# The gated experts' down products: from one f32 product to a sum of three f16 products

## What is computed

```python
# layer 1, "attention": a recurrence, one step for each token
h[t] = tanh(Wi @ ln(x[t]) + bi + Wh @ h[t-1] + bh);   x = x + h
# layer 1, ffn: one shared expert of 512 hidden columns and 16 routed ones of 64, 4 of them for a token
hidden = silu(xn @ gate) * (xn @ up)          # 1536 hidden columns in all
hidden[:, 512:] *= weight_of_the_token_for_the_expert   # 0 where it isn't chosen
x = x + hidden @ down                         # down: 1536 x 256
```

## Time and profile before

| what | us |
|---|---|
| median of three runs | 1479.22 (1477.72 to 1484.81) |
| the profiled execution | 1469.44 |
| its span, first to last instruction | 1467.7 |
| mean granted clock of PE | 0.987 |
| PE busy | 1420.8 (97%) |
| DVE busy | 806.5 (55%) |
| ACT busy | 594.2 (40%) |
| L1648, the down products, busy on PE | 113.4 |
| L535, fillers, busy on PE | 149.8 |

### The profile page before, as it was taken

How to read it: one execution, slowest core, us unless ns; L and a number is a source line. 1 busy time by engine, 2 the same in 40 slices (tenths; PEclk the granted TensorE clock), 3 DMA queues, 4 the chain that set the end, 5 groups by cost and what they waited for, 6 DMA issues and landing times.

```text
span 1467.7 us, 48130 instructions
## 1 busy us (share of the span) xinstructions
PE 1420.8 (97%) x19734; PEld 1006.2 (69%) x19734; DVE 806.5 (55%) x2574; ACT 594.2 (40%) x2778; POOL 38.0 (3%) x60
## 2 busy tenths in 40 slices
PE   5699899999999999999999999999999999999998
PEld 4466367777777777776776777777767677766555
DVE  6636864287854126967572225766444653455473
ACT  2052223734314784342248874551342334332310
POOL 1000000000000000000000000000000000000000
PEclk9799999999999999999999999999999999999999
DMA  5734100110000002110000002310000100002000
GB/s 160 143 79 107 38 2 2 23 41 3 2 2 3 2 4 43 35 25 3 2 3 3 3 3 90 94 25 1 2 2 15 39 3 2 16 2 38 16 1 15
DMA packets 45468, 40.17 MB, mean 27 GB/s; under 512 B 9723, under 2 KB 44486, under 8 KB 45254
## 3 DMA queue, kind: packets, MB, share of 16 engines
q1 hardware_dynamic: 43526, 36.32, 10.5%
q10 hardware_dynamic: 1728, 0.79, 0.5%
HBM read 25.81 MB, written 10.80 MB: 25 GB/s over the span
## 4 chain that ended last, share of the span: by engine, by line
PE 92%; DVE 4%; DMA 2%; SPq 1%; issue 0%; ACT 0%; DVEq 0%; ACTq 0%
PE b L516 22%; PE b L1596 9%; PE b L1376 9%; PE b L535 7%; PE b L1648 7%; PE b L1004 6%; PE b L975 5%; PE b L741 4%; PE b L920 4%; PE b L697 3%; DVE mx L929 3%; PE b L1257 2%; PE b L1232 2%; PE b L652 2%; PE b L1193 1%; PE b L459 1%
## 5 line engine op out<-in xcount | busy, mean ns | idle before, releaser
L516 PEld LDWEIGHTS b<-hp,whp 128*128 128x128 f16 x12276 | 482.2, 96 | 255.9 <-ACT hp L561 147.7
L516 PE MATMUL b<-hp,whp 128*128 128x2 f16 x12276 | 538.3, 165 | 1.8 <-ACT hp L561 0.5
L567 DVE TENSOR_TENSOR hp<-hist,hp 128x4 f16<-128x4 f32 x1023 | 165.5, 162 | 449.4 <-ACT hist L562 439.6
L561 ACT ACTIVATE hp<-b 128x4 f16<-128x4 f32 x1024 | 177.9, 174 | 511.5 <-PE b L516 499.2
L929 DVE TENSOR_REDUCE mx<-b 128x1 f32<-128x512 f32 (+3 forms) x304 | 188.3, 653 | 2.5 <-PE b L923 1.5
L989 ACT ACTIVATE vp<-b 128x512 f32<-128x512 f32 x288 | 170.8, 601 | 21.3 <-PE b L978 13.2
L562 ACT ACTIVATE hist<-b 128x4 f32<-128x4 f32 x1024 | 177.2, 173 | 0.0
L1596 PE MATMUL b<-vp,heads 128*128 128x512 f16 x576 | 159.9, 378 | 0.0
L535 PE MATMUL b<-whp 128*128 128x512 f16 (+7 forms) x562 | 149.8, 339 | 0.0
L1376 PE MATMUL b<-we,xT 128*128 128x256 f32 x512 | 147.7, 405 | 0.0
L920 PE MATMUL b<-heads 128*128 128x512 f16 (+3 forms) x384 | 112.6, 331 | 5.9 <-DVE mx L929 2.4
(11 more groups left out here) (203 smaller groups left out, 1573.4 us busy)
## 6 DMA issues: line engine op xcount, KB each, us to landing
x_qs<-qx_scr SPq DMA_DIRECT2D x48, 128.0 KB
qx_scr<-xq_pair SPq DMA_DIRECT2D x16, 256.0 KB, 2.1
heads<-q_scr SPq DMA_DIRECT2D x24, 128.0 KB, 4.4
heads<-k_scr SPq DMA_DIRECT2D x36, 64.0 KB, 2.6
x<-in_x SPq DMA_DIRECT2D x8, 256.0 KB, 6.4
q_scr<-tail SPq DMA_DIRECT2D x8, 256.0 KB, 2.3
k_scr<-tail SPq DMA_DIRECT2D x8, 256.0 KB, 2.3
we<-in_L_ffn_We SPq DMA_DIRECT2D x2, 1024.0 KB
```

Of the source, the lines that this page charges most:

```text
L516: return pe.matmul(self.z(t)[:, m], self.w.whp[:, a, k, m * P:(m + 1) * P], self.g.hp16[:, (t - 1) % 2, part, k, :], start=False, stop=Tru ...
L561: act.activation(self.g.hp16[:, t % 2, 0], self.z(t), ACT.Tanh, scale=1 / LIFT).then_inc(self.s["hi_ready"], 1)
```

## The change

A down product becomes three f16 products of 256 columns: high part of the hidden block with high part of `wd`, high with low, and low with high. `update` multiplies the sum by 1/64 while it adds. For each of the 48 blocks there are two new instructions: `keep_hidden` on ACT copies hT into its f16 high part, and `hidden_low` on DVE makes the f16 rest. The new pairs have three buffers `hp` in `heads`. `product` now waits for the block's `hidden_low` of three blocks before, and the new copy for its down products. The planner's cost for a down product goes from 0.43 to 0.33, with 0.52 and 0.6 for the new kinds.

The down matrix is loaded into another part of `heads` and split like the gate and up weights: four more `split_high` and four more `split_low`, 128x768 each.

Many semaphores that count one thing each are merged into a few (`filled`, `filled_v`, `prepared`, `ctx_in`), with the counts in the waits changed to match. Two waits change in what they wait for: the cast of the mask waits for all four loads of its group and not for the mask alone, and so does all that waited for three of them.

```diff
-        st.add("pe", "gat_down", self.down, n * MH * TC, 0.43, lambda i: rank(i // (MH * TC)) + 0.25,
+        st.add("act", "gat_hh", self.keep_hidden, n * MH, 0.52, of_block(0.245))
+        st.add("v", "gat_hl", self.hidden_low, n * MH, 0.6, of_block(0.246))
+        st.add("pe", "gat_down", self.down, n * MH * TC, 0.33, lambda i: rank(i // (MH * TC)) + 0.25,
...
     def product(self, v, i):
         if i >= 3:
-            v.wait_ge(self.s["down"], i - 2)
+            v.wait_ge(self.s["hl"], i - 2)
...
+    def keep_hidden(self, act, n):
+        c, m = self.blocks[n]
+        if m < MS:
+            act.wait_ge(self.s["hm"], n + 1)
+        else:
+            act.wait_ge(self.s["hc"], NR * c + m - MS + 1)
+        if n >= 3:
+            act.wait_ge(self.s["down"], n - 2)
+        act.activation(self.hp[:, n % 3, 0, :], self.hT[:, n % 3, :], ACT.Copy).then_inc(self.s["hh"], 1)
+
+    def hidden_low(self, v, n):
+        v.wait_ge(self.s["hh"], n + 1)
+        v.tensor_tensor(self.hp[:, n % 3, 1, :], self.hT[:, n % 3, :], self.hp[:, n % 3, 0, :], ALU.subtract
+                        ).then_inc(self.s["hl"], 1)
...
     def down(self, pe, i):
-        if p == 0 and m < MS:
-            pe.wait_ge(self.s["hm"], n + 1)
-        if p == 0 and m >= MS:
-            pe.wait_ge(self.s["hc"], NR * c + m - MS + 1)
-        last = pe.matmul(o[:, D * (p % 2):D * (p % 2) + D], self.hT[:, n % 3, P * p:P * p + P], self.w.wd[:, m, :],
-                         start=m == 0 and p % 2 == 0, stop=m == MH - 1, skip_group_check=True)
+        if i == 0:
+            pe.wait_ge(self.w.s["whole_split"], 12)
+        if p == 0:
+            pe.wait_ge(self.s["hl"], n + 1)
+        for at, (h, wd) in enumerate(((0, self.w.wd_hi), (0, self.w.wd_lo), (1, self.w.wd_hi))):
+            last = pe.matmul(o[:, D * (p % 2):D * (p % 2) + D], self.hp[:, n % 3, h, P * p:P * p + P], wd[:, m, :],
+                             start=m == 0 and p % 2 == 0 and at == 0, stop=m == MH - 1 and at == 2, skip_group_check=True)
...
     def update(self, v, j):
-        v.tensor_tensor(x, self.st.bank("gat_d", j // TC, p // 2)[:, D * (p % 2):D * (p % 2) + D], x, ALU.add
-                        ).then_inc(self.s["fx"], 1)
+        v.scalar_tensor_tensor(out=x, in0=self.st.bank("gat_d", j // TC, p // 2)[:, D * (p % 2):D * (p % 2) + D],
+                               scalar=1 / LIFT, in1=x, op0=ALU.mult, op1=ALU.add).then_inc(self.s["fx"], 1)
...
         def split_high(act, i):
+            if j == 2:
+                act.wait_ge(*w.gated_in)
+                act.activation(w.wd_hi[:, wd_part(i)], wd_whole[:, wd_part(i)], ACT.Copy, scale=LIFT
+                               ).then_inc(s["whole_high"], 1)
+                return
...
         def split_low(v, i):
+            if j == 2:
+                v.scalar_tensor_tensor(out=w.wd_lo[:, wd_part(i)], in0=wd_whole[:, wd_part(i)], scalar=LIFT,
+                                       in1=w.wd_hi[:, wd_part(i)], op0=ALU.mult, op1=ALU.subtract
+                                       ).then_inc(s["whole_split"], 1)
+                return
...
             if i == 2:
-                v.wait_ge(s["mask8_in"], 16)
-                v.tensor_copy(wx0.mask_row[:], mask8[:]).then_inc(s["mask_in"], 1)
+                v.wait_ge(s["ctx_in"], 64)
+                v.tensor_copy(wx0.mask_row[:], mask8[:]).then_inc(s["filled_v"], 1)
...
-        st.add("act", "split_high", split_high, 8, 0.8, lambda i: 1000)
-        st.add("v", "split_low", split_low, 8, 0.85, lambda i: 1000)
+        st.add("act", "split_high", split_high, 12, 0.8, lambda i: 1000)
+        st.add("v", "split_low", split_low, 12, 0.85, lambda i: 1000)
```

More of the change, by code:

```diff
@@ L1121, in rows_k @@
         sp.wait_ge(self.s["zeroed"], layer + 1)
-        sp.wait_ge(*w.rows_in)
+        for sem, count in w.rows_in:
+            sp.wait_ge(sem, count)
         rows = self.s[f"k_rows{layer}"]
@@ L1420, in __init__ @@
         self.ov = out.rearrange("(t p) d -> p t d", p=P)
-        self.s = st.sems("gat", "xh xl logits ex chain cT cph cpl cleared made th sv hm spread hc down fx stored")
+        self.s = st.sems("gat", "xh xl logits ex chain cT cph cpl cleared made th sv hm spread hc hh hl down fx stored")
         n = NK
@@ L1746, in all_layers @@
         wx1.bo, wx1.one_row, wx1.ones16 = sb("bo", [1, D]), sb("one_row", [1, P]), wx0.ones16
-        wx1.mask_in, wx1.rows_in, wx1.early = None, (s["rows"], 2), 200
+        wx1.mask_in, wx1.rows_in, wx1.early = None, wx0.rows_in, 200
         wx1.ctx_in, wx1.q_in, wx1.w_in = (s["ctx1_in"], 80), (s["q1_in"], 64), (s["q1_in"], 64)
-        w.wd, w.w_hi, w.w_lo = vp[:, 0:3072].rearrange("p (m n) -> p m n", m=MH), w_parts[0:2], w_parts[2:4]
+        w.wd_hi, w.wd_lo = (vp[:, 1536 * k:1536 * k + 1536].bitcast(F16).rearrange("p (m n) -> p m n", m=MH) for k in range(2))
+        w.w_hi, w.w_lo = w_parts[0:2], w_parts[2:4]
         w.gated_in = (s["w_in"], 48)
@@ L1962, in guard_cross @@
         def guard_cross(act):
-            act.wait_ge(s["lifted"], 1)
-            act.wait_ge(s["b_in"], 1)
-            act.wait_ge(s["w_lo"], 1)
+            act.wait_ge(s["prepared"], 3)
         def guard_rnn(act):
```

57 lines of the change are left out of this document (30 added, 27 removed).

## The result

The changed kernel takes 1461.32 us (median of six runs, 1454.39 to 1468.54) against 1478.84 us for the kernel before in the same comparison: a ratio of 0.9875, 95% interval 0.9833 to 0.9917. The profiled execution took 1454.39 us with a span of 1451.4. It is the fastest of the six, as the one before (1469.44) was faster than its median.

The account below looks back on a forecast made before the run. PE's queue, with down products on the recurrence's path, was taken as the bound after the standstill. Terms +5.5 - 15.7 + 1 - 3.2 = -12.4 us from the 1479.22 us median gave 1466.8 us, range 1456 to 1480.

Parts of the forecast that it names:

- Part 1: Start of the kernel, merged semaphores: the later cast of the mask is absorbed, 0 us, at most 1 us.
- Part 2: Standstill of the recurrence, waiting for layer 0's last chunk: added splits, copies and subtractions lengthen it 5.5 us (3.8 to 7.5).
- Part 3: 281 steps after the standstill: shorter down products on PE's queue, 293.1 to 277.4 us, -15.7 (-8 to -22).
- The low end of my range: 281 steps: only raw PE time goes and a third lands in gaps free anyway, -8 us.
- The new instructions: 23 ScalarE copies and 22 VectorE subtractions in the 281 steps: taken as 0, 7 us if the cover is gone.
- Part 4: Last step to last chunk's experts: five shorter blocks give -3.2 us, late work costs up to 4.1, sum +1.
- Part 5: Last chunk's experts: routing ends later but blocks are shorter, 56.5 to 53.3 us, -3.2 (-6 to -1).
- (b): Rival, no gain: the recurrence refills PE's gaps with fillers, -1.5 us in sum, 1478 us; chance 0.19.
- (a): Rival, bigger saving: all 281 steps reach their kind's shortest length, -22 us in sum, 1457 us; chance 0.15.
- (c): Rival, slower: new copies and subtractions delay the recurrence's tanh or subtraction, 1489 us at 0.5 us each; chance 0.07.
- (d): Rival, slower: weight loads can't overlap products, so a down product takes 0.61 us, 1504 us; chance 0.02.
- The median: Whole kernel: the change was put on the shown runs' median of 1479.22 us, giving 1466.8 us.

Follow-up runs that it names:

- sems_only: The kernel before with only the merged semaphores and their wait counts, down products still f32: 1482.4 us, ratio 1.0026.
- late_split: The changed kernel with the four down-matrix splits on ScalarE and VectorE ordered behind the last layer-0 chunk's highest-score reductions: 1457.01 us, ratio 0.9817.
- double_copies: The changed kernel, same order, with each keep_hidden copy and hidden_low subtraction issued twice, the extra into a spare buffer: 1487.71 us, ratio 1.0018.

## Why the prediction held, step by step

- **Part 1**, 0: right, shown by sems_only at full clock. The start's -4.1 us against the profile before is scatter: the profiles run here have their first step between 224.7 and 230.9 us.
- **Part 2**, +5.5: +4.7. The place was right, and of the 4.7 us that I gave the splits late_split shows 4.2. What I laid on top for the gated blocks' copies and subtractions was too much; between the splits and the standstill DVE sits idle 0.6 to 0.9 us in many of the steps, which is room for them.
- **Part 3**, -15.7: -17.0, and -18.3 at full clock. By classes: two f16 products in the long gap 27 x 0.955 (priced 0.98), the other 33 steps with down products 33.5 us (34), makes 93.2 (94.9), of which 1.4 is half clock, the rest 123.7 (122.1). The reason was right and is shown from both sides: the products alone in the old order give -12.6 us over 60 of 63 steps, and f32 products in the new order take 12.3 of the 17.0 back. The other 4.7 us are the order's, which the forecast held in its kinds of steps without naming it: there are fewer down products (88 for 94), and two together in the long gap cost 0.09 us less than one in each gap, 2.5 us over 27 steps. How the rest splits isn't measured. The low end of my range, raw time only, was no real bound: beside the recurrence an f32 product costs 0.148 us more, not 0.105.
- **The new instructions**, 0: right. 23 steps with the copy grew by 0.24 us in sum, 22 or 23 with the subtraction by 0.4 to 0.8, by how finely the kinds are cut, against the shortest step of their kind. The 0.16 us a copy was to cost in a step of 0.785 us did not come: three of the 23 copies stand in such steps, the others in steps of 0.84 us and more.
- **Part 4**, +1: +0.6, from two larger terms of opposite sign, as priced: the product alone gives -3.8 (priced -3.2), the copies, subtractions and the new order take 4.4 (4.1). How that splits between the three isn't measured.
- **Part 5**, -3.2: -2.7. The turn came at +22.5 us and the next down product at +28.0 (priced 22.5 and 28.3). The block was mis-sized: 4.32 us, not 4.20. The 1.84 us from L1648's start to the next makes already held the f32 weight load that I took off once more: the first of the eight f32 records starts 0.32 us ahead of the second, the others 0.216 from each other.
- **Rivals.** (b) would have needed the fillers to eat the gain: they did grow by 18.7 us, and the 281 steps became shorter all the same. (a) wanted 22 us in the 281 steps, where 17.0 came, 18.3 at full clock. The measured median lies about midway between the forecast and (a), but the forecast's terms each hold within 1.3 us. (c) and (d) fell in the runs above.
- **The median.** The time came out 5.5 us under the forecast, more than any part's error. The terms of the sum measured -14.4 in place of -12.4. Two stages that I had at 0 add -1.8: the start's scatter (-4.1) and the clock in the steps up to 740 (+2.3). Moving the difference of two profiles to the medians of a few runs adds the last 1.6: the spans differ by 16.3 and the medians by 17.5, and the kernel before was 1478.84 here and not 1479.22. That these went the same way is chance. That there was nothing to be had from the clock was read rightly off the stages of one profile, but half clock moves other runs of these kernels by more than any one of Parts 2, 4 and 5.

## What to carry to other kernels

Busy time of a product says little where another loop shares the engine: look for rows in which that loop holds exactly one, two or none of them, and price the change by the distance between the loop's rows. Don't take it that three products cost more than one: here an f16 product of 256 columns takes 0.109 us from start to start and an f32 one 0.43, and beside a run of tiny products the three were cheaper by 0.148 us, not by 0.105. When work is added for a conversion, ask first what stands behind it in each queue at the one place where everything waits: the four weight splits cost 4.2 us in front of the reductions and at most 0.5 behind them.

## What the hardware showed that I had not expected

**The scatter between runs goes with TensorE's clock.** In every profile the granted clock is 1.00 nearly everywhere, and 0.50 (1.2 in place of 2.4 GHz) in stretches of 3 to 21 us: in sum some 8 us behind 220 us in the kernel before, 22 in the changed one, 47 in sems_only, 69 in double_copies. Of the ten runs of the changed kernel those with mean clocks of 0.989 and 0.987 took 1453.5 and 1454.4 us, those with 0.973 and 0.974 took 1467.8 and 1468.5; of the kernel before, 0.986 took 1470.9, and 0.968 and 0.965 took 1492.2 and 1492.5. Over 52 runs of the kernel before in the three later comparisons, time and mean clock have a correlation of -0.95; one more took 6806.8 us at a clock of 1.00, and nothing here says why. The same instructions in the kernel before and in sems_only (L741 and L740), at full and at half clock:

```profile
1150.17 0.68 PE L741 MATMUL b<-xT,first 128*128 128x256 f32 x2
1150.68 0.44 PE L516 MATMUL b<-hp,whp 128*128 128x2 f16 x12
1150.99 0.68 PE L741 MATMUL b<-xT,first 128*128 128x256 f32 x2
```

```profile
1154.84 1.20 PE L740 MATMUL b<-xT,first 128*128 128x256 f32 x2
1155.84 0.51 PE L515 MATMUL b<-hp,whp 128*128 128x2 f16 x12
1156.20 1.20 PE L740 MATMUL b<-xT,first 128*128 128x256 f32 x2
```

A step is 1.36 us at half clock instead of 0.82. Windows of sems_only there (PE busy, then the clock as the third number from the end):

```profile
1148.00:1152.00 4.00, 3.89 (x75) 2.43 (x71) 1.91 (x10) 1.33 (x11) 0.69 (x1) 1.00 0.02 4
1152.00:1156.00 4.00, 3.89 (x69) 3.03 (x68) 1.74 (x7) 2.22 (x13) 0.00 (x0) 0.83 0.01 2
1156.00:1160.00 4.00, 4.00 (x44) 2.90 (x42) 0.49 (x3) 0.73 (x6) 0.00 (x0) 0.50 0.00 0
```

PE's records cover 3.89 of 4.00 us before it falls, just as in the kernel before at the same instructions, where it stays at 1.00. So neither the order nor the instructions decide it alone, and what decides it stays open. A stretch of 14 to 17 us costs 5 to 7 us in the recurrence, as much as Part 2 or more: whoever compares single profiles of such a kernel should compare the steps at full clock in both.

**Loads of 128x128 f16 weights pass every 0.056 us** beside products of 128 columns, where the earlier trace rows has six of them in 0.56 us: there products of 256 columns, 0.11 us apart, set the pace.
